# One down-projection group of the linear transformer behind the query projection, its last residual in pieces, and the quantised network's product added by GpSimd

## The chip, the core and the metric

The kernel runs on 1 core of one Trainium2 chip. A core has five engines that run their own instruction lists and meet at semaphores: TensorE (PE, matrix products; PEld is its weight load), VectorE (DVE), ScalarE (ACT), GpSimd (POOL) and SyncE (SP, here only DMA issue). The metric is the device time of one execution in microseconds (us). Lower is better.

## The reference, cut to what matters

The program is a chain of twelve sublayers on x (128 sequences of 32 tokens, width 128, so 4096 tokens). Two of them are touched.

Sublayer 2 is a linear transformer of 6 layers:

```python
for i in range(DEPTH):                       # DEPTH = 6
    xn = _layernorm(x, ln1_w[i], ln1_b[i])
    q, k, v = xn @ wq[i], xn @ wk[i], xn @ wv[i]      # split into 8 heads
    attn = softmax(q, axis=-1) @ (softmax(k, axis=-2).T @ v)
    x = attn @ wo[i] + bo[i] + x
    xn = _layernorm(x, ln2_w[i], ln2_b[i])
    hdn = xn @ w1[i]                         # 128 -> 512
    hdn = where(hdn >= 0, hdn, 0.01 * hdn)
    x = hdn @ w2[i] + x                      # 512 -> 128
```

and its result is added to the running x. Sublayer 9 is a two-layer network whose inputs, weights and biases are rounded to an integer grid: `h = relu(quant_linear(x, w1, b1)); x = x + quant_linear(h, w2, b2)`.

## The kernel before, in words

Everything is float32 except the integers of the quantised network, which are kept as bf16. The 4096 tokens are cut into CHUNKS = 8 chunks of 512 tokens (4 tiles of 128, TPC = 4).

**The linear transformer** (`linear_transformer`) is a hand-written software pipeline. Layers and chunks together make 48 items. One *step* starts an item (`now`), does the second part of attention of the item before it (`one`), the norm and feed-forward part of the one before that (`two`), and ends the feed-forward of the item three steps back (`three`). There are 48 steps that start an item and three more (48, 49, 50) that drain the pipe. The first 16 steps and the drain are written out, the other 32 run in a loop of two turns of 16 steps. Every engine has a function `step(now)` whose calls fix the order of its instructions; semaphores carry the dependences. SP only loads each layer's weights in this stage.

On PE the calls of a step are: `turn1` (4 transposes of the normed chunk into PSUM bank T), `down(three, 2)` (8 products of hidden block 2, lines L3090), `turn_keys`, `queries`, `turn_queries`, `keys`, `down(three, 3)`, `values`, `turn2`, `context`, `up` 0 and 1, `attend`, `up` 2, `down` 0, `up` 3, `down` 1, `attn_out`. All four transposing functions share the one PSUM bank T. ACT copies each of them out, and the next may write the bank only after that copy. For `turn_keys` this is the wait in its second and third line, on `s_hT1` of the item that `turn1` has just turned:

```python
def turn_keys(c):
    pe.wait_ge(s_k_exp, c.before + 1)
    if c.later(1).exists:
        pe.wait_ge(s_hT1, c.before + 2)
```

`queries` waits for the same copy, since it reads `hT1`. `down(c, 2)` waits for POOL's `leaky` (L2963), which adds two halves of the activation. POOL does it just after `apply1`, the norm of the following item (L2942, four tiles).

DVE ends the stage by adding the stream to X (`onto_x`, L3261): chunks 0 to 6 in one instruction in the last step (`now.at == 18`), chunk 7 behind everything.

**The quantised network** (`quantised_ffn`) ends in a loop over the 8 chunks. For each chunk DVE turns the hidden values of the next chunk into integers (`hidden_integers`, L2702), multiplies PE's result by the row of output scales into `product`, which has two buffers (L2706), and adds `product` to X (L2710). POOL adds the bias row to X for all 8 chunks (L2749), beginning when the rows are there. A barrier of all engines follows, and then the next cross attention (`t_cross`).

Of the kernel before, what the change touches and what calls it, by code (L numbers as in the profile page):

```python
# [13 lines left out]
ALU = mybir.AluOpType  # L14
# [11 lines left out]
TPC = 4  # L26
CHUNK = TPC * P
CHUNKS = TILES // TPC
# [150 lines left out]
def spread(ap, reps, axis):  # L179

    shape = list(ap.shape)
    shape.insert(axis, reps)
    return ap.unsqueeze(axis).to_broadcast(shape)
# [2438 lines left out]
def quantised_ffn(core, name, hT_all, quantised):  # L2622
# [7 lines left out]
    with Scope(core, name) as sc:  # L2630
# [4 lines left out]
        up, down = sc.sb("up", [P, NF * P], BF16), sc.sb("down", [P, NF * P], BF16)  # L2635
# [3 lines left out]
        diagonal, rows = sc.sb("diagonal", [P, 4, P]), sc.sb("rows", [P, 2, P])  # L2639
# [3 lines left out]
        product = sc.sb("product", [P, 2, TPC, P])  # L2643
# [4 lines left out]
        s_down, s_prod, s_bias, s_done = sc.sem("down"), sc.sem("prod"), sc.sem("bias"), sc.sem("done")  # L2648
# [5 lines left out]
        def tiles(c):  # L2654
            return X[:, c * TPC:(c + 1) * TPC]

        @block.vector
        def _(dve):
# [44 lines left out]

            def add(c):
                dve.wait_ge(s_down, c + 1)
                dve.tensor_tensor(product[:, c % 2], psum[:, D_BANK + c % 2].rearrange("p (k d) -> p k d", k=TPC),  # L2706
                                  spread(rows[:, 0], TPC, 1), ALU.mult).then_inc(s_prod, 1)
                dve.wait_ge(s_prod, c + 1)
                dve.wait_ge(s_bias, c + 1)
                dve.tensor_tensor(tiles(c), product[:, c % 2], tiles(c), ALU.add).then_inc(s_done, 1)  # L2710

            link(dve.tensor_reduce(peak[:, 0:1], quantised.peaks[:], AX.X, ALU.max))
            whole_maximum(0, 255.0)
# [19 lines left out]
            for c in range(CHUNKS):  # L2733
                if c + 1 < CHUNKS:
                    hidden_integers(c + 1)
                add(c)
            dve.wait_ge(s_done, CHUNKS)

        @block.gpsimd
        def _(pool):  # L2740
            core.clear_used(pool)
            for c in range(CHUNKS):
                pool.wait_ge(s_shift, c + 1)
                if c >= 2:
                    pool.wait_ge(s_up, NF * (c - 1))
                pool.tensor_scalar(x_int[:, c % 2], shifted[:, c % 2], ROUND, None, ALU.subtract).then_inc(s_x_int, 1)
            pool.wait_ge(s_rows, 1)
            for c in range(CHUNKS):
                pool.tensor_tensor(tiles(c), tiles(c), spread(rows[:, 1], TPC, 1), ALU.add).then_inc(s_bias, 1)  # L2749

        @block.tensor
        def _(pe):
# [52 lines left out]
def linear_transformer(core, name, stream, slots):  # L2805
# [9 lines left out]
    with Scope(core, name) as sc:  # L2815
# [36 lines left out]
        tiles = lambda ap: ap.rearrange("p (t c) -> p t c", c=P)  # L2852
# [138 lines left out]
        def _(pe):  # L2991
            def turn1(c):
                pe.wait_ge(s_norm1, c.before + 1)
                if c.later(-3).exists:
                    pe.wait_ge(s_hT2, c.before - 2)
                elif c.later(-2).exists:
                    pe.wait_ge(s_qT, 1)
                elif c.later(-1).exists:
                    pe.wait_ge(s_hT1, 1)
                for t in range(TPC):  # L3000
                    last = pe.transpose(psum[:, T_BANK, t * P:(t + 1) * P], Y1[:, t], ident)
                last.then_inc(s_turn1, 1)
# [5 lines that stand above are left out]
                else:  # L3008
                    pe.wait_ge(s_hT2, c.before - 1)
                for t in range(TPC):  # L3010
                    last = pe.transpose(psum[:, T_BANK, t * P:(t + 1) * P], k[:, c.n % 2, t * P:(t + 1) * P], ident)
                last.then_inc(s_k_turn, 1)

            def turn_queries(c):
                pe.wait_ge(s_soft, c.before + 1)
                pe.wait_ge(s_k_tok, c.before + 1)
                for t in range(TPC):
                    last = pe.transpose(psum[:, T_BANK, t * P:(t + 1) * P], q[:, c.n % 2, t * P:(t + 1) * P], ident)
                last.then_inc(s_q_turn, 1)
# [11 lines left out]
            def queries(c):  # L3031
                pe.wait_ge(s_hT1, c.before + 1)
                pe.wait_ge(s_q_less, c.before)
                for t in range(TPC):
                    last = pe.matmul(psum[:, Q_BANK, t * P:(t + 1) * P], hT1[:, t * P:(t + 1) * P], c.attn(0), start=True, stop=True)
                last.then_inc(s_qp, 1)

            def keys(c):
                pe.wait_ge(s_k_less, c.before)
                pe.matmul(psum[:, K_BANK], c.attn(P), hT1[:], start=True, stop=True).then_inc(s_kp, 1)  # L3040
# [44 lines left out]
            def down(c, f):  # L3085
                pe.wait_ge((s_early, s_late)[f // 2], c.before * 2 + f % 2 + 1)
                if f == 0 and c.later(-1).exists:
                    pe.wait_ge(s_layer, c.before)
                for t in range(TPC):
                    last = pe.matmul(psum[:, D_BANK, t * P:(t + 1) * P], hidden[:, f, t * P:(t + 1) * P], c.ffn((NF + f) * P),  # L3090
                                     start=(f == 0 and t == 0), stop=(f == NF - 1 and t == TPC - 1))
                if f == NF - 1:
                    last.then_inc(s_down, 1)

            def step(now):
                one, two, three = now.later(-1), now.later(-2), now.later(-3)
                if now.exists:
                    turn1(now)
                if three.exists:
                    down(three, 2)  # L3100
                if one.exists:
                    turn_keys(one)
                if now.exists:
                    queries(now)
                if one.exists:
                    turn_queries(one)
                if now.exists:
                    keys(now)
                if three.exists:
                    down(three, 3)  # L3110
                if now.exists:
                    values(now)
                if two.exists:
                    turn2(two)
                if one.exists:
                    context(one)
                if two.exists:
                    up(two, 0)
                    up(two, 1)
                if one.exists:  # L3120
                    for t in range(TPC):
                        attend(one, t)
                if two.exists:
                    up(two, 2)
                    down(two, 0)
                    up(two, 3)
                    down(two, 1)
                if one.exists:
                    attn_out(one)
# [65 lines left out]
        def _(dve):  # L3195
# [57 lines left out]
            def ffn_added(c):  # L3253
                dve.wait_ge(s_down, c.before + 1)
                dve.tensor_tensor(c.chunk(), tiles(psum[:, D_BANK]), c.chunk(), ALU.add).then_inc(s_layer, 1)

            def onto_x(first, last):

                at = slice(first * TPC, last * TPC)
                dve.wait_ge(s_layer, (DEPTH - 1) * CHUNKS + last)  # L3260
                dve.tensor_tensor(X[:, at], X[:, at], stream[:, at], ALU.add)  # L3261

            def step(now):
                one, two, three, following = now.later(-1), now.later(-2), now.later(-3), now.later(1)
                if two.exists:
                    attention_added(two)
                    statistics(1, two, s_stats2, s_moments2, s_norm2)
                if now.exists:
                    soften(now, Q_BANK, q, q_stat, DH, s_qp, s_q_top, s_q_less)
                if two.exists:  # L3270
                    apply2(two)
                if now.exists:
                    soften(now, K_BANK, k, k_stat, S, s_kp, s_k_top, s_k_less)
                    totals(now, q, q_stat, DH, s_q_exp, s_q_sum, s_q_inv, s_soft)
                if one.exists:
                    own_context(one)
                if following.exists:
                    statistics(0, following, s_stats1, s_moments1, s_norm1)
                if isinstance(now.i, int) and now.at == 2 * CHUNKS + 2:
                    onto_x(0, CHUNKS - 1)  # L3280
                if three.exists:
                    ffn_added(three)
                if two.exists:
                    leaky(two, 0)
                    leaky(two, 1)
                if now.exists:
                    totals(now, k, k_stat, S, s_k_exp, s_k_sum, s_k_inv, s_unit)

            statistics(0, Step(0, 0), s_stats1, s_moments1, s_norm0)
            steps(dve, step, lambda i, side: None)  # L3290
            onto_x(CHUNKS - 1, CHUNKS)
        sc.close_block()


# [229 lines left out]
```

## Time and profile before

| what | value |
|---|---|
| time, median of 3 runs | 3991.93 us (3991.15 to 3996.01) |
| the profiled execution's own time | 3982.57 us |
| its span, first to last instruction | 3980.8 us |
| PE, PEld, DVE, ACT, POOL busy | 85%, 62%, 67%, 59%, 61% |
| mean granted TensorE clock | 0.925 of full speed |
| linear transformer, first transposes to the last add | 544 us to 1336.7 us |
| quantised network, last loop | 2850.0 us to 2875.0 us |

The two stages are read apart, since another engine bounds each. A row of the timeline has the start and the length in us, the engine, the line, the operation, what it writes and reads, and in brackets the idle time before it and what ended it. Rows of one line that follow each other closely are merged, with their count behind the x; a merged row's length is from the start of the first to the end of the last. PE work overlaps, so the time that a group of products takes on PE is read from its start to the next group's start.

### The profile page before, as it was taken

What the parts mean: (1) busy time and instruction counts of PE and PEld (TensorE: products, weight loads), DVE (VectorE), ACT (ScalarE), POOL (GpSimd) and SP (SyncE); (2) the same over time, 40 slices, a digit from 0 to 9 for tenths busy, and PEclk for the clock granted to TensorE, in tenths of its full rate; (3) what the DMA queues carried; (4) which work ended last, traced back from release to release, by engine and by line L of the source; (5) the groups of instructions that cost most, each with busy time, mean ns of one, the idle gap of its engine ahead of it and who ended that gap; (6) DMA issues with size and microseconds to landing.
All of it is one profiled execution on the core that took longest, in us unless ns stands there. A gap on an engine that the chain in (4) does not pass through costs nothing. (4 is left out here: it accounts for less than half of the span.)

```text
span 3980.8 us, 119953 instructions
## 1 busy us (share of the span) xinstructions
PE 3385.2 (85%) x44674; PEld 2469.3 (62%) x44674; DVE 2670.8 (67%) x7002; ACT 2362.3 (59%) x6308; POOL 2422.3 (61%) x2724
## 2 busy tenths in 40 slices
PE   7999959999999579698698999978499999786866
PEld 5777737777777467365466777745277777453444
DVE  6888757777777523477445888857778887754655
ACT  6777736666666334386124777745577777644633
POOL 6767656776777343574425887746367676845733
PEclk9999979999999689898799999989599999887968
DMA  2111110000000122101221111110011111000023
GB/s 75 36 42 36 36 70 6 8 11 11 8 6 2 63 72 77 47 14 47 67 72 59 51 45 42 37 60 4 17 37 36 42 36 30 3 2 6 2 93 94
DMA packets 90549, 149.05 MB, mean 37 GB/s; under 512 B 10112, under 2 KB 66816, under 8 KB 89664
## 3 DMA queue, kind: packets, MB, share of 16 engines
q1 hardware_dynamic: 79936, 122.87, 9.9%
q0 software_dynamic: 10240, 20.99, 1.7%
q8 instruction: 261, 4.28, 0.4%
q14 instruction: 112, 0.92, 0.1%
HBM read 112.76 MB, written 31.06 MB: 36 GB/s over the span
## 5 line engine op out<-in xcount | busy, mean ns | idle before, releaser
L2251 POOL TENSOR_TENSOR t_cross_E<-t_cross_E,t_cross_inverse 128x1028 f32<-128x1028 f32 x128 | 243.2, 1900 | 134.8 <-DVE t_cross_inverse L2530 134.8
L2251 POOL TENSOR_TENSOR a_cross_E<-a_cross_E,a_cross_inverse 128x1028 f32<-128x1028 f32 x128 | 243.2, 1900 | 132.8 <-DVE a_cross_inverse L2530 132.8
L2477 ACT ACTIVATE t_cross_E<-t_cross_psum,t_cross_negtop 128x257 f32<-128x257 f32 x512 | 238.8, 472 | 113.5 <-DVE t_cross_negtop L2520 110.0
L2477 ACT ACTIVATE a_cross_E<-a_cross_psum,a_cross_negtop 128x257 f32<-128x257 f32 x512 | 238.8, 472 | 112.4 <-DVE a_cross_negtop L2520 103.9
L2477 ACT ACTIVATE e_cross_E<-e_cross_psum,e_cross_negtop 128x257 f32<-128x257 f32 x512 | 238.8, 472 | 111.2 <-DVE e_cross_negtop L2520 103.3
L2251 POOL TENSOR_TENSOR e_cross_E<-e_cross_E,e_cross_inverse 128x1028 f32<-128x1028 f32 x128 | 243.2, 1900 | 94.2 <-DVE e_cross_inverse L2530 94.1
L3090 PEld LDWEIGHTS l_psum<-l_ffn_w,l_hidden 128*128 128x128 f32 x1536 | 197.9, 192 | 98.0 <-issue 56.1
L3090 PE MATMUL l_psum<-l_ffn_w,l_hidden 128*128 128x128 f32 x1536 | 207.8, 278 | 19.0 <-POOL l_hidden L2963 17.9
L3083 PE MATMUL l_psum<-l_hT,l_ffn_w 128*128 128x512 f32 x384 | 200.6, 625 | 0.9 <-ACT l_hT L3139 0.9
L2520 DVE TENSOR_REDUCE t_cross_negtop<-t_cross_psum 128x2 f32<-128x514 f32 x256 | 175.8, 687 | 32.6 <-PE t_cross_psum L2337 31.7
L2520 DVE TENSOR_REDUCE a_cross_negtop<-a_cross_psum 128x2 f32<-128x514 f32 x256 | 175.4, 686 | 26.8 <-PE a_cross_psum L2332 26.4
L2520 DVE TENSOR_REDUCE e_cross_negtop<-e_cross_psum 128x2 f32<-128x514 f32 x256 | 175.6, 686 | 24.6 <-PE e_cross_psum L2332 24.5
L2942 POOL TENSOR_SCALAR l_normed<-inner,l_moments,l_rstd 128x128 f32<-128x128 f32 x192 | 149.8, 793 | 14.8 <-POOL l_rstd L2936 14.8
L2390 PE MATMUL e_cross_psum<-const_sb,e_cross_E 128*128 128x128 f32 x1024 | 154.3, 274 | 0.2
L2390 PE MATMUL a_cross_psum<-const_sb,a_cross_E 128*128 128x128 f32 x1024 | 153.4, 273 | 0.2
L2390 PE MATMUL t_cross_psum<-const_sb,t_cross_E 128*128 128x128 f32 x1024 | 153.4, 273 | 0.2
L2953 POOL TENSOR_TENSOR l_q<-l_q,l_q_stat 128x512 f32<-128x512 f32 x48 | 50.8, 1058 | 167.3 <-DVE l_q_stat L3217 167.3
L2963 POOL TENSOR_TENSOR l_hidden<-l_hidden,l_less 128x512 f32<-128x512 f32 x96 | 122.2, 1293 | 18.2 <-ACT l_hidden L3163 18.2
L1467 POOL DMA_INDIRECT slots<-hT_all,behind_place_i x64 | 61.7, 965 | 111.5 <-PE c_moe_psum L1600 61.9
L1467 POOL DMA_INDIRECT slots<-inner,a_moe_place_i x64 | 62.0, 969 | 101.6 <-PE a_moe_psum L1600 59.0
L3237 DVE TENSOR_TENSOR inner<-l_psum,inner 128x512 f32<-128x512 f32 x48 | 33.2, 692 | 132.1 <-PE l_psum L3075 132.1
L2390 PEld LDWEIGHTS e_cross_psum<-const_sb,e_cross_E 128*128 128x128 f32 x1024 | 121.2, 142 | 0.9 <-ACT e_cross_ET L2467 0.4
(754 smaller groups left out, 11124.1 us busy)
## 6 DMA issues: line engine op xcount, KB each, us to landing
a_cross_context<-context SPq DMA_DIRECT2D x32, 578.0 KB, 3.7
e_cross_context<-context SPq DMA_DIRECT2D x32, 578.0 KB, 3.7
t_cross_context<-context SPq DMA_DIRECT2D x32, 578.0 KB, 3.7
u_moe_weights<-pack_u_moe SPq DMA_DIRECT2D x1, 5633.0 KB, 16.3
slots<-l_blank SPq DMA_DIRECT2D x6, 832.0 KB, 12.2
a_moe_x_slots<-slots SPq DMA_DIRECT2D x26, 192.0 KB, 2.8
slots<-a_moe_y_slots SPq DMA_DIRECT2D x26, 192.0 KB, 2.1
c_moe_x_slots<-slots SPq DMA_DIRECT2D x26, 192.0 KB, 2.8
```

What stands on the lines that cost most here:

```text
L1467: pool.indirect_dma_start(slots.halves[g], bass.IndirectOffsetOnAxis(ap=place_i[:, k, at:at + 1], axis=0), rows[:, at], None).then_inc(s_p ...
L2251: pool.tensor_tensor(E[:, n % N], E[:, n % N], spread(inverse[:, n % 4], SK, 2), ALU.mult).then_inc(s_unit, 1)
L2390: last = pe.transpose(psum[:, (T_BANK, K_BANK)[c], g * P:(g + 1) * P], E[:, n % N, g, c * P:(c + 1) * P], ident)
L2477: act.activation(E[:, n % N, g], psum[:, g, 0:SK], ACT.Exp, bias=negtop[:, n % 2, g:g + 1], accum_out=total[:, n % 2, g:g + 1]).then_inc(s ...
L2520: dve.tensor_reduce(negtop[:, n % 2, at], psum[:, at, 0:SK], AX.X, ALU.max, negate=True).then_inc(s_top, 1)
L2942: last = pool.tensor_scalar(Y1[:, t], c.tile(t), moments[:, 0, t, 0:1], rstd[:, 0, 1, t:t + 1], ALU.subtract, ALU.mult)
L2953: pool.tensor_tensor(groups, groups, spread(q_stat[:, 2], DH, 2), ALU.mult).then_inc(s_soft, 1)
L2963: pool.tensor_tensor(hidden[:, f], hidden[:, f], less[:, f - 2], ALU.add).then_inc(s_late, 1)
L3083: pe.matmul(psum[:, U_BANKS[f % 2]], c.ffn(f * P), hT2[:], start=True, stop=True).then_inc(s_up, 1)
L3090: last = pe.matmul(psum[:, D_BANK, t * P:(t + 1) * P], hidden[:, f, t * P:(t + 1) * P], c.ffn((NF + f) * P), start=(f == 0 and t == 0), st ...
L3237: dve.tensor_tensor(c.chunk(), tiles(psum[:, C_BANK]), c.chunk(), ALU.add).then_inc(s_mid, 1)
```

## The change

It has three parts.

1. On PE `down(three, 2)` stands behind `queries(now)` instead of behind `turn1(now)`. In steps 3 to 47 all of these calls exist. No semaphore changes.
2. DVE adds the stream to X in four pieces of two chunks: three of them in steps 48, 49 and 50, the fourth at the end.
3. In the quantised network DVE no longer adds `product` to X. POOL does, and the bias of chunk c + 1 is added ahead of the product of chunk c. DVE's multiplication now waits until POOL has used the product of two chunks back.

```diff
@@ quantised_ffn
             def add(c):
                 dve.wait_ge(s_down, c + 1)
+                if c >= 2:
+                    dve.wait_ge(s_done, c - 1)
                 dve.tensor_tensor(product[:, c % 2], psum[:, D_BANK + c % 2].rearrange("p (k d) -> p k d", k=TPC),
                                   spread(rows[:, 0], TPC, 1), ALU.mult).then_inc(s_prod, 1)
-                dve.wait_ge(s_prod, c + 1)
-                dve.wait_ge(s_bias, c + 1)
-                dve.tensor_tensor(tiles(c), product[:, c % 2], tiles(c), ALU.add).then_inc(s_done, 1)
...
             pool.wait_ge(s_rows, 1)
+            pool.tensor_tensor(tiles(0), tiles(0), spread(rows[:, 1], TPC, 1), ALU.add).then_inc(s_bias, 1)
             for c in range(CHUNKS):
-                pool.tensor_tensor(tiles(c), tiles(c), spread(rows[:, 1], TPC, 1), ALU.add).then_inc(s_bias, 1)
+                if c + 1 < CHUNKS:
+                    pool.tensor_tensor(tiles(c + 1), tiles(c + 1), spread(rows[:, 1], TPC, 1), ALU.add).then_inc(s_bias, 1)
+                pool.wait_ge(s_prod, c + 1)
+                pool.wait_ge(s_bias, c + 1)
+                pool.tensor_tensor(tiles(c), product[:, c % 2], tiles(c), ALU.add).then_inc(s_done, 1)
+            pool.wait_ge(s_done, CHUNKS)
@@ linear_transformer, PE
                 if now.exists:
                     turn1(now)
-                if three.exists:
-                    down(three, 2)
                 if one.exists:
                     turn_keys(one)
                 if now.exists:
                     queries(now)
+                if three.exists:
+                    down(three, 2)
                 if one.exists:
                     turn_queries(one)
@@ linear_transformer, DVE
-                if isinstance(now.i, int) and now.at == 2 * CHUNKS + 2:
-                    onto_x(0, CHUNKS - 1)
+                if isinstance(now.i, int) and 2 * CHUNKS <= now.at < 2 * CHUNKS + 3:
+                    onto_x(2 * (now.at - 2 * CHUNKS), 2 * (now.at - 2 * CHUNKS) + 2)
...
-            onto_x(CHUNKS - 1, CHUNKS)
+            onto_x(CHUNKS - 2, CHUNKS)
```

On PE, at the head of a step in the linear transformer, before (L3001 `turn1`, L3090 `down`, L3011 `turn_keys`, L3035 `queries`, L3018 `turn_queries`, L3040 `keys`):

```order
L3001 MATMUL l_psum<-const_sb,l_normed 128x128 x4
L3090 MATMUL l_psum<-l_ffn_w,l_hidden 128x128 x4
L3011 MATMUL l_psum<-const_sb,l_k 128x128 x4
L3035 MATMUL l_psum<-l_attn_w,l_hT 128x128 x4
L3018 MATMUL l_psum<-const_sb,l_q 128x128 x4
L3040 MATMUL l_psum<-l_hT,l_attn_w 128x512
```

And now, with lines four further on:

```order
L3005 MATMUL l_psum<-const_sb,l_normed 128x128 x4
L3015 MATMUL l_psum<-const_sb,l_k 128x128 x4
L3039 MATMUL l_psum<-l_attn_w,l_hT 128x128 x4
L3094 MATMUL l_psum<-l_ffn_w,l_hidden 128x128 x4
L3022 MATMUL l_psum<-const_sb,l_q 128x128 x4
L3044 MATMUL l_psum<-l_hT,l_attn_w 128x512
```

Nothing stands between `turn1` and `turn_keys` any more, and the products of `down` are between `queries` and `turn_queries`.

On POOL, at the end of the quantised network, before (the x8 bias adds are one row):

```order
L2746 TENSOR_SCALAR q_ffn_x_int<-q_ffn_shifted 128x512 x8
L2749 TENSOR_TENSOR X<-X,q_ffn_rows 128x512 x8
L168 UNCONDITIONAL_BRANCH
L2228 UNCONDITIONAL_BRANCH
L2288 MEMSET t_cross_last_of 128x256
```

And now (L2752 adds a product, L2746 and L2749 a bias; the last seven rows before the next stage):

```order
L2752 TENSOR_TENSOR X<-q_ffn_product,X 128x512
L2749 TENSOR_TENSOR X<-X,q_ffn_rows 128x512
L2752 TENSOR_TENSOR X<-q_ffn_product,X 128x512
L2749 TENSOR_TENSOR X<-X,q_ffn_rows 128x512
L2752 TENSOR_TENSOR X<-q_ffn_product,X 128x512 x2
L168 UNCONDITIONAL_BRANCH
L2228 UNCONDITIONAL_BRANCH
```

POOL has 16 additions of a chunk where it had 8, and the last one stands directly ahead of the barrier.

On DVE, in the last steps of the linear transformer, now (L3265 is `onto_x`, L3259 the add of the feed-forward part; before, one row of 128x3584 and one of 128x512 stood around the last L3255):

```order
L3226 TENSOR_TENSOR l_ctx<-l_psum,l_unit 128x512
L3265 TENSOR_TENSOR X<-X,inner 128x1024
L3259 TENSOR_TENSOR inner<-l_psum,inner 128x512
L3254 SCALAR_TENSOR_TENSOR l_hidden<-l_hidden 128x512 x2
L3241 TENSOR_TENSOR inner<-l_psum,inner 128x512
L3231 BN_STATS l_stats<-inner 128x6 x4
L3235 BN_AGGR l_moments<-l_stats 128x2 x4
L3248 TENSOR_SCALAR l_normed<-inner,l_moments,l_rstd 128x128 x4
L3265 TENSOR_TENSOR X<-X,inner 128x1024
L3259 TENSOR_TENSOR inner<-l_psum,inner 128x512
```

Two more pieces of the same width follow, around the last L3259.

## Rows read from the trace of the kernel before

**Rows 1.** Windows: busy us (and count) of PE, PEld, DVE, ACT, POOL; granted clock

```profile
592.00:1302.00 710.00, 690.66 (x10888) 535.66 (x10886) 513.53 (x1486) 444.93 (x765) 505.98 (x586) 1.00 0.03 7
2850.00:2876.00 26.00, 14.07 (x128) 12.22 (x128) 24.47 (x25) 12.34 (x6) 15.55 (x9) 0.57 0.00 1
```

**Rows 2.** Timeline of PE in a settled step (start, length)

```profile
907.06 0.60 PE L3001 MATMUL l_psum<-const_sb,l_normed 128*128 128x128 f32 x4
908.03 1.16 PE L3090 MATMUL l_psum<-l_ffn_w,l_hidden 128*128 128x128 f32 x8 [0.38 <-POOL l_hidden L2963]
909.03 0.60 PE L3011 MATMUL l_psum<-const_sb,l_k 128*128 128x128 f32 x4
...
922.89 0.60 PE L3001 MATMUL l_psum<-const_sb,l_normed 128*128 128x128 f32 x4
```

**Rows 3.** Timeline of ACT and POOL in the same step

```profile
907.70 0.78 ACT L3139 ACTIVATE l_hT<-l_psum,l_attn_w 128x512 f32<-128x512 f32 x1 [0.80 <-PE l_psum L3001]
...
919.46 3.12 POOL L2942 TENSOR_SCALAR l_normed<-inner,l_moments,l_rstd 128x128 f32<-128x128 f32 x4 [0.31 <-POOL l_rstd L2936]
```

**Rows 4.** Timeline of PE in step 17, where POOL is early

```profile
812.71 0.60 PE L3001 MATMUL l_psum<-const_sb,l_normed 128*128 128x128 f32 x4
...
814.27 0.63 PE L3011 MATMUL l_psum<-const_sb,l_k 128*128 128x128 f32 x4
814.73 1.06 PE L3035 MATMUL l_psum<-l_attn_w,l_hT 128*128 128x128 f32 x8
815.68 0.63 PE L3018 MATMUL l_psum<-const_sb,l_q 128*128 128x128 f32 x4
...
817.00 1.05 PE L3090 MATMUL l_psum<-l_ffn_w,l_hidden 128*128 128x128 f32 x8
817.89 1.06 PE L3045 MATMUL l_psum<-l_attn_w,l_hT 128*128 128x128 f32 x8
...
827.96 0.60 PE L3001 MATMUL l_psum<-const_sb,l_normed 128*128 128x128 f32 x4
```

**Rows 5.** Timeline of PE: `turn1` of steps 3, 32 and 47

```profile
591.52 0.66 PE L3001 MATMUL l_psum<-const_sb,l_normed 128*128 128x128 f32 x4
...
1050.40 0.65 PE L3001 MATMUL l_psum<-const_sb,l_normed 128*128 128x128 f32 x4 [2.25 <-issue]
...
1285.72 0.60 PE L3001 MATMUL l_psum<-const_sb,l_normed 128*128 128x128 f32 x4
```

**Rows 6.** Timeline of DVE and POOL while the linear transformer drains

```profile
1314.06 1.27 POOL L2963 TENSOR_TENSOR l_hidden<-l_hidden,l_less 128x512 f32<-128x512 f32 x1 [8.26 <-ACT l_hidden L3163]
...
1327.83 3.89 DVE L3261 TENSOR_TENSOR X<-X,inner 128x3584 f32<-128x3584 f32 x1
...
1329.46 4.60 POOL L2963 TENSOR_TENSOR l_hidden<-l_hidden,l_less 128x512 f32<-128x512 f32 x2 [9.42 <-ACT l_hidden L3163]
...
1335.31 0.69 DVE L3255 TENSOR_TENSOR inner<-l_psum,inner 128x512 f32<-128x512 f32 x1 [3.59 <-PE l_psum L3090]
1336.04 0.69 DVE L3261 TENSOR_TENSOR X<-X,inner 128x512 f32<-128x512 f32 x1
```

**Rows 7.** Timeline of POOL in the quantised network: all eight, then two alone

```profile
2850.52 15.24 POOL L2749 TENSOR_TENSOR X<-X,q_ffn_rows 128x512 f32<-128x512 f32 x8 [12.80 <-DVE q_ffn_rows L2731]
2852.79 1.29 POOL L2749 TENSOR_TENSOR X<-X,q_ffn_rows 128x512 f32<-128x512 f32 x1
2855.71 2.26 POOL L2749 TENSOR_TENSOR X<-X,q_ffn_rows 128x512 f32<-128x512 f32 x1
```

**Rows 8.** Timeline of DVE in the quantised network

```profile
2854.55 2.28 DVE L2702 TENSOR_SCALAR q_ffn_h_int<-q_ffn_rounded 128x2048 bf16<-128x2048 f32 x1
2856.75 0.68 DVE L2706 TENSOR_TENSOR q_ffn_product<-q_ffn_psum,q_ffn_rows 128x512 f32<-128x512 f32 x1
...
2866.24 1.21 DVE L2702 TENSOR_SCALAR q_ffn_h_int<-q_ffn_rounded 128x2048 bf16<-128x2048 f32 x1
...
2874.34 0.69 DVE L2710 TENSOR_TENSOR X<-q_ffn_product,X 128x512 f32<-128x512 f32 x1
```

More of the change, by code:

```diff
@@ L2736, in _ @@
                 add(c)
-            dve.wait_ge(s_done, CHUNKS)
         @block.gpsimd
```

## The prediction

> **What bounds the kernel.** I read the windows first. In the linear transformer PE is busy 690.66 of 710 us at the full granted clock, 2.4 GHz, and no other engine passes 514 us [rows 1]: there a microsecond of PE is a microsecond of the kernel. In the last loop of the quantised network it is DVE, busy 24.47 of 26 us, with POOL at 15.55 [rows 1]. So the first part of the change is judged on PE, the third on the port that DVE and POOL share.
>
> Then the timeline of one settled step of the linear transformer. It lasts 922.89 - 907.06 = 15.83 us, and its visible flaw is the wait of PE for POOL's `l_hidden` ahead of `down`, 0.38 us [rows 2]. What the reader is to see is that another wait lies under it. `turn_keys` starts at 909.03, but it may not start before ACT has copied out what `turn1` left in the same PSUM bank. ACT begins that at 907.70 and takes 0.78 us, to 908.48 [rows 3]. So in the settled step POOL is the later releaser, and ACT's copy is only half a microsecond behind.
>
> Step 17 shows the same head with POOL early. `down` is issued at once behind `turn1`, and `turn_keys` still starts 814.27 - 812.71 = 1.56 us after `turn1` [rows 4]. The eight products of `down` fill that hole. This step lasts 827.96 - 812.71 = 15.25 us, the shortest of the stage: it is what PE needs when nobody but ACT's copy holds it up.
>
> **Part 1, `down` behind `queries`.** It removes nothing; PE issues the same products. The hole of 1.56 us between `turn1` and `turn_keys` stays, since its cause is ACT and not POOL, and is now empty. The products of `down` become a piece of their own behind `queries`. Eight of them take 817.89 - 817.00 = 0.89 us from their start to the next group's [rows 4]. Against that, `turn_queries` now has them as cover for ACT's copy of the keys: in step 17 it came 815.68 - 814.73 = 0.95 us behind `queries`, where eight products need 0.89, so 0.06 is saved [rows 4]. The new step is 15.25 + 0.89 - 0.06 = 16.08 us if PE sets it.
>
> It does, for nothing else comes late. POOL's `l_hidden` is now needed 2 us later. `queries`, and all that DVE and POOL do behind it, start at 1.56 + 0.46 = 2.02 us into the step (0.46 from `turn_keys` to `queries` [rows 4]), not at 909.03 + 0.44 - 907.06 = 2.41. POOL's norm for the next `turn1` ended at 919.46 + 3.12 = 922.58, 0.31 us before it was used [rows 3]; it gains up to 0.39 from the earlier start and 0.25 from the longer step. DVE's norm for `turn2` is earlier too while PE comes to it later. So the loop over DVE and POOL, which set the step before, has slack, and PE's own list sets it.
>
> From step 3 to step 47 there are 44 intervals, 1285.72 - 591.52 = 694.20 us, 15.78 each [rows 5]. In that sum are starts of the loop body that no order on PE changes: 2.25 us of issue at step 32 [rows 5], and I put as much as 1.1 us more on the entries at steps 3 and 16 (an estimate: half of the one seen). The new sum is 44 x 16.08 + 3.35 = 710.9, so +16.7 us, and the 45th step of this kind adds 0.3: **+17.0 us**. In the drain `turn_keys` gets ahead of `down`, but the next step then waits for POOL's deviation, which nothing moved: 0.
>
> Bounds: if the hole is 1.62 and DVE or POOL take back what they gain, the step is 16.2 us, +22. If the step rises only from the settled 15.83 by the difference of the hole and its two old fillings, 15.83 - (909.03 - 907.06) + 1.56 + 0.89 - 0.22, with 0.22 for small waits before `turn_queries` and `turn2` that go, it is 16.09 again; with each of these waits taken at 0.3 it would be 15.9, +9.
>
> **Part 2, the residual in pieces.** DVE's 3.89 us add over seven chunks runs from 1327.83, and POOL's two `l_hidden` additions beside it take 4.60 us from 1329.46, where one alone took 1.27 [rows 6]. PE's last `down` and DVE's last two adds hang on them. With pieces of two chunks, 0.69 + (3.89 - 0.69) / 6 = 1.22 us each [rows 6], the third piece ends at 1329.05, before POOL begins. POOL's pair then takes between 2 x 1.27 = 2.54 and, since its second half waits for ACT, some 3.3 us: 1.3 to 2.1 earlier; I take 1.3. The last piece is 1.22 long and not 0.69, +0.5. The pieces in steps 48 and 49 lie where DVE waits for POOL and ACT. Sum **-0.7 us**, between -1.5 and +0.6 (cover gone in step 48, no gain at the end).
>
> **Part 3, GpSimd adds the product.** Per chunk DVE loses an add of 0.69 us [rows 8], and POOL gains one of 1.29 [rows 7]. That alone would suit DVE, but the two engines hinder each other. The integer step takes DVE 2.28 us while POOL works and 1.21 alone; the multiplication that reads PSUM takes 0.68 us with POOL at work [rows 8]; POOL's addition takes 1.29 alone and 2.26 when an integer step falls on it [rows 7]. So each integer step costs POOL 2.26 - 1.29 = 0.97 us.
>
> Before, POOL's eight additions were over at 2850.52 + 15.24 = 2865.76, and DVE ended undisturbed at 2874.34 + 0.69 = 2875.03. Now POOL has 16 additions, one behind the other. Rows of it overlap by some 0.05, so 16 x 1.24 = 19.8 us, and seven integer steps fall among them (DVE's multiplication waits for POOL's add of two chunks back, which keeps the two in step): 7 x 0.97 = 6.8. The first product is ready before POOL wants it. At the end two additions wait on a multiplication for 0.3 at most. End: 2850.52 + 26.6 + 0.3 = 2877.4 to 2877.9, against 2875.03. The next stage begins behind the barrier, and all of it moves: **+2.7 us**. Bounds: no interference, 16 x 1.24, is -4.7; every addition at 2.26 is 36.2 us, +11.7. I stay near the middle, since integer steps fall on just under half of the additions.
>
> The Trainium skill has a rule against this part: GPSIMD Engine Reference, 4.1 Engine selection, puts an elementwise operation with two inputs on VectorE, GpSimd being about twice as slow. The trace agrees: 1.29 to 0.69 us, a factor of 1.87 [rows 7, 8]. It also says (SBUF — State Buffer, the section on the two separate sides) that the port pair of the two engines is locked for a whole instruction and the other blocks. By it each integer step would cost POOL its full 1.21 us and not 0.97, an estimate of 1.7 us more; the row says a little less than the rule.
>
> **Sum.** 17.0 - 0.7 + 2.7 = +19.0 us on the profiled execution's 3982.57, which is 4001.6. The runs' median of 3991.93 lies 9.4 us above that execution; the difference is carried over unchanged: **4010.9 us**, 0.48% slower. Less than 0.2%, 8 us, could not be told from no change here.
>
> **Rivals.**
> (a) *The loop through POOL sets the step, and `down` leaves it.* For: PE waits for POOL's `l_hidden` in every settled step [rows 2]; with `down` behind `queries`, the queries start 0.4 us earlier, and the chain DVE, POOL, `down`, `turn_keys`, `queries`, DVE gets shorter by 1.0 us. If the hole behind `turn1` then counted for nothing, all steps would come down to step 17's 15.25: 44 x 15.25 + 3.35 - 694.2 = -20 us, with the other parts 3974 us. It decides if `turn_keys` starts less than about 1.2 us behind `turn1`. Against: step 17, where POOL is early and the hole is 1.56 all the same [rows 4]. 6 in 100.
> (b) *The price is there but small.* The step comes to 15.9 us (+5 to +9) and part 3 to its lower bound because POOL and DVE fall apart in time: 3991.93 + 7 - 0.7 - 3 = 3995. For: a settled step holds small waits I can't see one by one. 12 in 100.
> (c) *The granted clock.* PE's idle share rises from 3% to some 8%; in the quantised network, where PE is busy about half the time, the clock stood at 0.57 [rows 1]. At 1.2 GHz a step's 15 us of PE work nearly double, so even three steps are +45: about 4055 us. Against: in step 17's head, and in the 2.25 us at step 32, no row slows. 4 in 100.
> (d) The change does what it says by the instruction order, so a change without effect is only (b).
>
> **Chances and range.** My forecast has 78 in 100. Its own range is +10 to +25 us, from the step's bounds and part 3's nearer ones. To hold 8 in 10 the range takes in some of (b): 3998 to 4023. Faster 0.07: (a) and a bit. Same 0.13: (b) and the lower edge. Slower 0.80.
>
> **What would show it.** In the new profile `turn_keys` should start 1.55 to 1.6 us behind `turn1` with PE idle about 1.0 us before it, released by ACT's `l_hT`; no wait for POOL's `l_hidden` ahead of `down`; `turn1` every 16.0 to 16.15 us, the same in both halves of the loop body. POOL's two additions in the drain should take about 3.3 us together and the last one of the quantised network end near 2877.7 plus the shift. I am wrong if the step is below 15.9 us, if PE's hole is filled, or if the clock's row for 592 to 1302 falls below 1.00.

## The result, and the profile after

| | before | after |
|---|---|---|
| time, median of 5 runs | 3991.93 us (3990.57 to 3996.01) | 4015.23 us (4012.67 to 4016.09) |
| ratio to before, 95% interval | | 1.0054 (1.004 to 1.0069) |
| the profiled execution's own time | 3982.57 us | 4015.23 us |
| settled step of the linear transformer | 15.83 / 15.65 us | 16.07 us |
| `turn1` of step 3 to `turn1` of step 47 | 694.20 us | 712.67 us |
| that `turn1` to the end of the last add | 51.01 us | 50.66 us |
| POOL's first addition to its end, quantised network | 24.51 us (DVE's end) | 26.63 us |

The change costs 23.3 us; 19.0 had been forecast. The three lower rows explain +18.5, -0.35 and +2.1 of the profiled executions. These two executions lie 32.7 us apart, since the one of before was 9.4 us under its median. Most of the rest is in stages with no edit (`c_self` +4.7, `retention` +4.0, `t_cross` +3.3); e3, which does not touch `c_self` either, has it 3.4 us longer than before. I do not read it.

One profile of each kernel is also a thin basis for the first two of these, 694.20 to 712.67 and 51.01 to 50.66. The profile of before is the fastest of its kind in both. Where nothing in the linear transformer differs from before, the 44 intervals take 694.20 us in before, 698.65 in e3 and 695.51 in e8 (the experiments are below), and the stretch behind them takes 51.01, 52.57 and 52.46.

The timeline of PE in a settled step after the change (start, length, engine, line; in brackets the idle time and what ended it):

```profile
916.14 0.60 PE L3005 MATMUL l_psum<-const_sb,l_normed 128*128 128x128 f32 x4
917.70 0.63 PE L3015 MATMUL l_psum<-const_sb,l_k 128*128 128x128 f32 x4 [0.96 <-ACT l_hT L3143]
918.17 1.06 PE L3039 MATMUL l_psum<-l_attn_w,l_hT 128*128 128x128 f32 x8
919.06 1.06 PE L3094 MATMUL l_psum<-l_ffn_w,l_hidden 128*128 128x128 f32 x8
919.95 0.60 PE L3022 MATMUL l_psum<-const_sb,l_q 128*128 128x128 f32 x4
...
932.21 0.60 PE L3005 MATMUL l_psum<-const_sb,l_normed 128*128 128x128 f32 x4
```

These answer to [rows 2]. The wait for POOL's `l_hidden` is gone; in its place is one of 0.96 us for ACT's `l_hT`. `turn_keys` still starts 1.56 us behind `turn1`, as in [rows 4]. `down(three, 2)` now takes 0.89 us of its own behind `queries`, 919.06 to 919.95. The step is 932.21 - 916.14 = 16.07 us, in both halves of the loop body.

Windows of after (columns as in [rows 1]): the stage, a piece of step 32, a piece of the drain, and the last loop of the quantised network.

```profile
593.00:1321.00 728.00, 681.46 (x10885) 533.04 (x10885) 520.68 (x1485) 439.44 (x765) 505.37 (x586) 1.00 0.03 7
1064.40:1067.80 3.40, 3.40 (x18) 3.40 (x18) 0.85 (x2) 0.60 (x1) 1.65 (x2) 0.50 0.00 0
1325.00:1333.00 8.00, 6.12 (x162) 3.82 (x166) 4.45 (x9) 1.97 (x3) 0.67 (x1) 0.79 0.01 2
2880.00:2906.00 26.00, 11.99 (x123) 10.24 (x121) 15.49 (x15) 11.64 (x6) 26.00 (x16) 0.63 0.01 1
```

PE's idle share in the stage rose from 2.7% to 6.4%, and the granted clock is still 1.00 as a mean of the stage. It was not 1.00 all the time: for 3.4 us of step 32 it was 0.50, the 1.2 GHz level, and it fell once more in the drain. In the last loop the bound moved from DVE, busy 24.47 of 26 us [rows 1], to POOL, busy all 26.

The timeline of DVE and POOL there, one chunk of the settled part and the end, answers to [rows 7, 8]:

```profile
2886.52 1.28 POOL L2749 TENSOR_TENSOR X<-X,q_ffn_rows 128x512 f32<-128x512 f32 x1
2886.68 0.69 DVE L2708 TENSOR_TENSOR q_ffn_product<-q_ffn_psum,q_ffn_rows 128x512 f32<-128x512 f32 x1 [1.24 <-POOL X L2752]
2887.28 1.61 DVE L2702 TENSOR_SCALAR q_ffn_h_int<-q_ffn_rounded 128x2048 bf16<-128x2048 f32 x1
2887.76 2.27 POOL L2752 TENSOR_TENSOR X<-q_ffn_product,X 128x512 f32<-128x512 f32 x1
2889.98 1.28 POOL L2749 TENSOR_TENSOR X<-X,q_ffn_rows 128x512 f32<-128x512 f32 x1
...
2903.97 2.48 POOL L2752 TENSOR_TENSOR X<-q_ffn_product,X 128x512 f32<-128x512 f32 x2
```

An addition with an integer step on it takes 2.27 us, one with only the multiplication on it 1.28. DVE waits 1.24 us in each chunk for POOL to free a `product` buffer.

### The profile page after: what moved, and what is told of

The parts are those of the page before. It is cut to its first block and busy times, and to the rows that moved or that the text cites. A ratio compares the mean times of both kernels' runs of the same rounds, so it can differ in the third digit from the quotient of the medians.

```text
span 4013.4 us, 119960 instructions
## 1 busy us (share of the span) xinstructions
PE 3390.0 (84%) x44673; PEld 2470.8 (62%) x44674; DVE 2671.4 (67%) x6996; ACT 2357.3 (59%) x6308; POOL 2431.1 (61%) x2732
## 5 line engine op out<-in xcount | busy, mean ns | idle before, releaser
L2520 DVE TENSOR_REDUCE a_cross_negtop<-a_cross_psum 128x2 f32<-128x514 f32 x256 | 175.4, 686 | 26.9 <-PE a_cross_psum L2332 26.6
L2390 PEld LDWEIGHTS t_cross_psum<-const_sb,t_cross_E 128*128 128x128 f32 x1024 | 121.2, 142 | 1.0 <-ACT t_cross_ET L2467 0.4
```

The source lines that it names most:

```text
L2390: last = pe.transpose(psum[:, (T_BANK, K_BANK)[c], g * P:(g + 1) * P], E[:, n % N, g, c * P:(c + 1) * P], ident)
L2520: dve.tensor_reduce(negtop[:, n % 2, at], psum[:, at, 0:SK], AX.X, ALU.max, negate=True).then_inc(s_top, 1)
```

## The experiments

Kernels with the same number under "before there" ran on one chip together with those runs of before; the ratio is to them.

| kernel | median us | before there | ratio (95%) | settled step us |
|---|---|---|---|---|
| e1 order alone | 4011.69 | 3994.37 | 1.0045 (1.0031 to 1.0058) | 16.06 |
| e2 pieces alone | 3988.34 | 3994.37 | 0.9987 (0.9977 to 0.9996) | 15.83 / 15.65 |
| e3 POOL adds alone | 3997.02 | 3994.37 | 1.0008 (0.9999 to 1.0017) | not touched |
| e4 block 2 on DVE | 3978.73 | 3994.37 | 0.9958 (0.9945 to 0.9972) | 15.25 |
| e5 filler of transposes | 4071.98 | 4003.64 | 1.017 (1.0156 to 1.0184) | 16.06 to 19.84 |
| e6 `turn1` ahead | 4034.63 | 4003.64 | 1.0073 (1.0059 to 1.0087) | 16.33 / 16.14 |
| e7 e4 with pieces | 3988.61 | 4003.64 | 0.9961 (0.9947 to 0.9975) | 15.25 |
| e8 no bias adds | 3990.41, one run | 4003.64 | none | not touched |
| e9 filler, one product | 4014.95 | 3990.01 | 1.006 (1.0048 to 1.0072) | 16.07 |
| e10 16 empty instructions | 4073.68 | 3990.01 | 1.0212 (1.0198 to 1.0227) | 16.06 to 19.92 |
| e11 e7 with the order | 4010.89 | 3990.01 | 1.0052 (1.0039 to 1.0065) | 16.06 |
| e12 12 empty instructions | 4025.33 | 4004.2 | 1.005 (1.0033 to 1.0067) | 16.06 |

**e1, e2, e3: each part by itself.** The edits are the three parts of the diff, one at a time.

> Kernel before with part 1 alone (down block 2 behind the query projection). Theory A (the hole between turn1 and turn_keys is ACT's copy and is now empty): turn1 every 16.07 us as in the changed kernel, linear transformer +18 to +19 us, total +17 to +20 us. Theory B (part 1 costs less and the rest of the +23 us comes from part 3's effect on later stages): total +10 us or less.

> Kernel before with part 2 alone (residual in four pieces). Theory A: POOL's last two additions take about 3.3 us together and not 4.6, the stage ends 0.7 us earlier; total within 1 us of before, not to be told from no change. Theory B (the pieces hold up DVE in the drain): the stage ends up to 1 us later.

> Kernel before with part 3 alone (GpSimd adds the product). Theory A (POOL's 16 additions in a row and the port shared with DVE's integer steps): last loop of the quantised network +2 to +3 us, total +2 to +3. Theory B (later stages, above all the cross attention behind it, are slower because of it): total +6 us or more. Theory C (DVE is freed and this pays): -2 us or better.

Part 1 alone gives +17.3 us and the step of 16.06: the cost is the order on PE. Part 2 gives -6.0 by the medians. Its own rows show less: from `turn1` of step 47 to the last add it takes 49.08 us, against 51.01 in before and 52.57 in e3, so -1.9 to -3.5. The other 2.5 to 4 us are in no row that it touches. Part 3 gives +2.6, with an interval that just takes in none; its last loop has the same 26.6 us as after. The three sum to +14, and together they measured +23. By the ratios (+0.45, -0.13, +0.08% against +0.54%) the 0.14% between them is within the intervals, so I do not call it an interaction.

**e4: take POOL's lateness away and leave `down` in the hole.** On before: hidden block 2 goes through DVE, as 0 and 1 do; ACT writes it in one copy, and POOL keeps block 3 alone.

```diff
@@ POOL                                    @@ DVE, behind totals(now, k, ...)
-                    leaky(two, 2)          +                    leaky(two, 2)
@@ PE down                                  @@ ACT raw
-  s_early / s_late by f // 2               -                if f >= 2:
+  s_early for f < 3, s_late for f == 3     +                if f == 3:
```

> Kernel before, down left where it was, but the activation of hidden block 2 made by DVE (after its key totals, where it waits for PE) as for blocks 0 and 1, so that ACT writes one copy of it and POOL handles block 3 alone. Theory A (the 0.53 us hole behind turn1 was POOL's lateness, and ACT's copy of 1.56 us is the next limit): a step falls from 15.74 us on average to 15.3 to 15.5, total -11 to -20 us. Theory B (the loop over DVE sets the step): DVE's 0.69 us more make a step as long or longer, total 0 to +10 us.

This is the version that beats both kernels, by 0.42% under before. Its head of a step, in the timeline of PE:

```profile
920.01 0.60 PE L3000 MATMUL l_psum<-const_sb,l_normed 128*128 128x128 f32 x4
920.44 1.06 PE L3092 MATMUL l_psum<-l_ffn_w,l_hidden 128*128 128x128 f32 x8
921.57 0.63 PE L3010 MATMUL l_psum<-const_sb,l_k 128*128 128x128 f32 x4
```

`down` follows at once, `turn_keys` still comes at 1.56 us, and every undisturbed step takes 15.25. So the wait for POOL that one sees in [rows 2] was worth 0.4 to 0.6 us a step, and was to be had without emptying the hole. The edit also takes a copy from ACT and an addition from POOL; how much of the gain belongs to each was not tried.

**e7 and e11: with and without the order, where POOL is never late.** e7 is e4 with part 2; e11 adds part 1 to it.

> Block 2's activation on DVE (as in e4_block2_dve) and the residual in pieces (part 2), the rest as before. Theory A (the two gains are in different places and add up): step 15.25 us, total -15 to -22 us on before. Theory B (part 2's gain in its own run was chance): as e4_block2_dve, -15.6 us within 3.

> e7_block2_dve_pieces with part 1 on top (down block 2 behind the queries). There PE never waits for POOL at the head of a step, so the price of the place stands alone. Theory A (0.89 us of work leaves a place where it was free): step 15.25 to 16.05 us, +35 to +38 us on e7_block2_dve_pieces, so +19 to +22 us on before. Theory B (part 1's price is tied to POOL's lateness): +17 us or less on e7_block2_dve_pieces.

The step goes from 15.25 to 16.06, +0.81, where the prediction's terms have 0.89 - 0.06 = 0.83. e7 cannot be told from e4. Against their own runs of before, e7 is 15.0 us faster and e11 20.9 us slower: where POOL is never late, the order costs about 36 us and not 17, since before had already paid POOL's lateness. In e11 the hole is there although POOL is early:

```profile
934.67 0.60 PE L3000 MATMUL l_psum<-const_sb,l_normed 128*128 128x128 f32 x4
936.23 0.63 PE L3010 MATMUL l_psum<-const_sb,l_k 128*128 128x128 f32 x4 [0.96 <-ACT l_hT L3141]
```

**e5, e9, e10, e12: is the hole free?** Each puts something between `turn1` and `turn_keys` of after: e5 eight transposes into a bank that is free then, e9 one 128x512 product into it, e10 and e12 no work but 16 or 12 semaphore increments.

```diff
@@ e5: after turn1(now)
+                for n in range(2):
+                    for t in range(TPC):
+                        pe.transpose(psum[:, Q_BANK, t * P:(t + 1) * P], Y1[:, t], ident)
@@ e9
+                pe.matmul(psum[:, Q_BANK], ident, Y1[:].rearrange("p t c -> p (t c)"), start=True, stop=True)
@@ e10; e12 has range(12)
+                for n in range(16):
+                    pe.sem_inc(passed_pe, 1)
```

> The changed kernel with eight more transposes on PE between turn1 and turn_keys in each of the 48 steps (they read turn1's source, write the query bank and are overwritten by the queries; 0.88 us of PE work). Theory A (PE stands idle there until ACT's copy lands): the step stays at 16.07 us within 0.05, total as the changed kernel within 3 us, so +17 to +26 us on before. Theory B (the step is the length of PE's own list, or the products of down got dearer at their new place): 16.95 us a step, total +60 us and more on before.

> The changed kernel with one more product of 128x512 on PE between turn1 and turn_keys (two matmuls and two weight loads with one wait: some 0.9 us of PE work in 5 instructions, where e5_filler had 0.88 us in 17); overwritten by the queries. Theory A1 (the place is idle; e5_filler's loss was the supply of PE's instructions, seen as 0.9 to 2 us gaps for which the profile names no releaser): settled step 16.07 us, few such gaps, total +15 to +35 us on before. Theory A2 (work there is not free): +60 us or more.

> The changed kernel with 16 instructions that only raise an unused count, on PE between turn1 and turn_keys: no PE work, but as many more instructions in a step as e5_filler. Theory A1 (instruction supply): the 0.9 to 2 us gaps of e5_filler come back, total +40 to +70 us on before. Theory B1 (PE work in the place is what e5_filler paid for): as the changed kernel, +17 to +26 us.

> The kernel after with 12 semaphore increments in the hole between turn1 and turn_keys, where the run before it had 16 and cost 1.6% over the kernel after. PE issues some 498 instructions a step (966 products and weight loads and 31 others in two steps of the trace), so this makes it about 510 and the 16 made it 514. Theory A, a boundary: the instruction list comes in packets of 16384 bytes, two in a step, and what fits in them costs nothing, so the step stays 16.07 us, few issue gaps, 0 to +8 us over the kernel after (ratio to before 1.005 to 1.008). Theory B, a price for each instruction: 12/16 of 59 us, +44 us over the kernel after, ratio 1.016 to 1.018, with some 25 issue gaps ahead of the small products of attend. A value between 1.009 and 1.015 would fit neither.

e5 missed what the theory of a free hole said: +1.7%. e9 shows that the theory holds all the same: about 0.9 us of work in each step, the settled step is still 16.07 us, and the ratio to before is 1.006, where after has 1.0054. What e5 had besides work was instructions, and e10, with instructions and no work, costs more than e5. The timeline of PE in e10, at three steps one after the other (`attend` is L3075, 128 products a step):

```profile
691.78 1.25 PE L3075 MATMUL l_psum<-l_qT,l_ctx 32*32 32x32 f32 x125
694.31 0.25 PE L3075 MATMUL l_psum<-l_qT,l_ctx 32*32 32x32 f32 x3 [1.27 <-issue]
...
709.33 1.27 PE L3075 MATMUL l_psum<-l_qT,l_ctx 32*32 32x32 f32 x126
711.90 0.24 PE L3075 MATMUL l_psum<-l_qT,l_ctx 32*32 32x32 f32 x2 [1.30 <-issue]
...
726.92 1.27 PE L3075 MATMUL l_psum<-l_qT,l_ctx 32*32 32x32 f32 x127
730.10 0.21 PE L3075 MATMUL l_psum<-l_qT,l_ctx 32*32 32x32 f32 x1 [1.92 <-issue]
```

The reader is to see the counts: the wait falls behind 125, 126, 127 products. It moves on by one product, a weight load and a matmul, in each step. Counting all of PE's records, a step of e10's written-out part has 510, and the waits lie at records 15441, 15953 and 16465: 512 apart each time. Up to the second turn of the loop the other waits of over 0.6 us in e10 (but one, in step 2) and in e5 lie whole multiples of 512 from these, within two records. Those of after, e1, e2, e3 and e11 (18257 in all five) and e9 are whole multiples of 512 apart too, but half of 512 away from those of e10, which nothing here explains. In the loop's second turn they come back at the same places of the body. So PE can run dry at every 512th record, and in its longest waits within a settled step the ones ahead of it are the dense small products of `attend`. Not every such place has a wait: steps 4 and 6 of e10 have none.

A second loss comes with the first. In each step of e5 and e10 from step 2 on that takes over 19 us (five and eight of them) the granted clock also fell from 2.4 to 1.2 GHz for a few microseconds. So what e5 and e10 lost is not the waits alone.

e12's result fits its theory A (ratio 1.005, no wait of that kind in the loop's steady part), but the reason that it gives, fewer than 512 in a step, is not the whole one. Its loop steps have 511 records, so the 512th stays at nearly the same place of each step, and that place is not in `attend`; e10's have 515, and it drifts slowly through the end of `attend`. Before and after have 494 in the written-out steps and 499 in the loop, so the place moves on by 18 or 13 records a step; besides the loop's second turn such waits show in steps 13 to 15 alone, one in before and in after, two or three in e1, e2 and e3. e9's loop has 503, with waits of 1.3 to 1.4 us in the steps 21, 34 and 37, and of 0.36 us in step 18.

That this is the supply of instructions is argued: the queue named "instruction" moved 1.46 MB in 89 packets in some 44 steps of before, two of 16 KB in a step. It was not tried by itself, nor is it shown why a wait at a given record comes in one execution and not in the next.

**e6: another order that fills the hole.** On after, `turn1` of the next item stands ahead of `attn_out`, whose eight products cover ACT's copy.

```diff
-                if now.exists:
-                    turn1(now)
...
+                if now.later(1).exists:
+                    turn1(now.later(1))
                 if one.exists:
                     attn_out(one)
```

> The changed kernel with the next item's turn1 ahead of the attention's output projection, so that real work (0.89 us) lies in the hole. Theory A: the step falls from 16.07 to 15.5 to 15.9 us (15.2 by PE's list, but POOL's norm is ready only some 15.5 us into the step and DVE gets the output projection later), total +0 to +13 us on before. Theory B (the hole is not what costs): the step stays at 16.07, total +20 us or more.

A miss. The hole is gone, but the step is 16.33 and 16.14 us. The timeline of PE and DVE:

```profile
843.69 0.66 PE L3005 MATMUL l_psum<-const_sb,l_normed 128*128 128x128 f32 x4 [0.47 <-POOL l_normed L2946]
844.18 1.06 PE L3079 MATMUL l_psum<-l_attn_w,l_aT 128*128 128x128 f32 x8
845.30 0.63 PE L3015 MATMUL l_psum<-const_sb,l_k 128*128 128x128 f32 x4
...
845.27 0.69 DVE L3242 TENSOR_TENSOR inner<-l_psum,inner 128x512 f32<-128x512 f32 x1 [3.79 <-PE l_psum L3079]
```

DVE gets the attention's result 1.58 us behind `turn1`, where e7 has 934.30 - 934.10 = 0.20. All that DVE and POOL do behind it is later, and PE waits for POOL's norm at the next `turn1`. The order moved the bound to the loop over DVE and POOL. The total, +31 us on before, is what theory B gave, but not for its reason, since the hole is filled.

**e8: how much of part 3 is POOL's second addition.** Part 3 on before, with POOL's bias adds left out.

```diff
-            pool.tensor_tensor(tiles(0), tiles(0), spread(rows[:, 1], TPC, 1), ALU.add).then_inc(s_bias, 1)
...
-                if c + 1 < CHUNKS:
-                    pool.tensor_tensor(tiles(c + 1), tiles(c + 1), spread(rows[:, 1], TPC, 1), ALU.add).then_inc(s_bias, 1)
...
-                pool.wait_ge(s_bias, c + 1)
```

> Part 3 alone, with POOL's eight additions of the bias row left out (the down bias is missing from the output). Theory A (POOL's 16 additions in a row are the length of the last loop): the loop is then DVE's, 8 integer steps of 1.2 to 2.3 us and 8 multiplications of 0.68, 16 to 20 us from the rows' arrival to the last addition where part 3 alone takes 26.6. Theory B (each DVE-POOL round trip of product and buffer is what costs): the loop stays above 23 us.

Its POOL, in the timeline:

```profile
2868.30 14.43 POOL L2748 TENSOR_TENSOR X<-q_ffn_product,X 128x512 f32<-128x512 f32 x7 [14.99 <-DVE q_ffn_product L2708]
2883.14 1.26 POOL L2748 TENSOR_TENSOR X<-q_ffn_product,X 128x512 f32<-128x512 f32 x1 [0.41 <-DVE q_ffn_product L2708]
```

The stage, from PE's first weight load to the first instruction of the next one, takes 59.47 us against 67.78 with part 3 whole (e3) and 65.71 before. From the rows' arrival to the last addition it is 18.4 us where e3 takes 26.7, inside theory A's 16 to 20. With eight additions POOL is no longer the bound: it waits for DVE's last product. So what costs is 16 additions on one engine. Without the bias, adding the product on POOL would gain 65.71 - 59.47 = 6.2 us; that is an upper bound, since here nobody adds the bias. The single time of 3990.41 us is not read.

## Why the prediction was right, and where its terms were off

**The order, and the sum's largest term.** Predicted 16.08 us for the step, measured 16.07, in both halves as said; the hole is 1.56 us with 0.96 idle. That POOL is not the cause is shown by e11, where POOL is early and the hole stays, and that PE stands idle in it by e9, where work in it costs nothing. That it is ACT's copy of `l_hT` is read from the wait in the code and from the releaser in the profile; no run makes the copy shorter or gives `turn_keys` a bank of its own. The 44 intervals came to 712.67 us against 710.9. 44 x 16.07 is 707.1, so the disturbed steps hold 5.6 us and not the 3.35 that I carried over from before: 17.57 at step 14, where a wait of 1.30 us for issue stands behind 123 of `attend`'s products, and 17.95 and 17.96 at steps 31 and 32. The wait of 1.72 us for issue at the start of step 32 is the excess of step 31. The excess of step 32 itself is the clock, as the timeline of PE shows:

```profile
1062.62 0.65 PE L3005 MATMUL l_psum<-const_sb,l_normed 128*128 128x128 f32 x4 [1.72 <-issue]
1064.23 0.94 PE L3015 MATMUL l_psum<-const_sb,l_k 128*128 128x128 f32 x4 [0.96 <-ACT l_hT L3143]
1064.97 1.91 PE L3039 MATMUL l_psum<-l_attn_w,l_hT 128*128 128x128 f32 x8
```

Behind the wait for issue and the hole, 1.72 and 0.96 us idle with `turn1` alone between them, eight products take 1.91 us and not 1.06, and the window 1064.40 to 1067.80 shows 0.50. Before had a longer wait at this place, 2.25 us [rows 5], no hole behind it, no fall, and a step of 15.30. e1 and e11, with the order, have 17.96 and 17.75; e9, with the hole filled, has no fall and 16.12. A full hole does not always prevent it: e2 and e7, which keep `down` there, fell too, with 16.60 and 17.13.

That was the mis-sized term, +2.3 us. "Starts of the loop body that no order on PE changes" was the sentence that failed: one of these waits is no start of the body at all, the empty hole adds a fall of the clock to another, and they differ between executions. For the last reason the 18.5 us are themselves uncertain. With the order of before the 44 intervals take 694.2 to 698.7 us (before, e2, e3, e8, mean 696.4), with that of after 712.7 to 715.3 (after, e1, e11, mean 714.2): +17.8, where +16.7 was forecast.

**The pieces and the drain.** Their row in the first table was forecast at -0.4 (-0.7 for the pieces, +0.3 for the 45th step, nothing else from the order) and measured -0.35. That this agrees is luck: both terms were too small, and before's profile is the fastest of its kind here. POOL's last two additions, in after:

```profile
1349.96 1.56 POOL L2967 TENSOR_TENSOR l_hidden<-l_hidden,l_less 128x512 f32<-128x512 f32 x1 [8.47 <-ACT l_hidden L3167]
1351.71 1.26 POOL L2967 TENSOR_TENSOR l_hidden<-l_hidden,l_less 128x512 f32<-128x512 f32 x1 [0.19 <-ACT l_hidden L3167]
...
1354.95 1.23 DVE L3265 TENSOR_TENSOR X<-X,inner 128x1024 f32<-128x1024 f32 x1
```

They take 3.01 us from the first start to the last end, where 3.3 was said and 4.60 stood before [rows 6]: 1.6 gained, less the 0.5 for the longer last piece. In other profiles with the residual in one instruction the pair takes longer than in before, and most in e1, whose timeline of DVE and POOL has:

```profile
1349.95 3.88 DVE L3261 TENSOR_TENSOR X<-X,inner 128x3584 f32<-128x3584 f32 x1
1350.75 5.43 POOL L2963 TENSOR_TENSOR l_hidden<-l_hidden,l_less 128x512 f32<-128x512 f32 x2 [8.47 <-ACT l_hidden L3163]
```

e1 and after differ in this stage by the pieces alone, and agree up to the last step's `turn2` within 0.02 us. From `turn1` of step 47 to the last add they take 53.61 and 50.66 us: the pieces gain 2.95. e2 against before gives 1.9 and against e3 3.5, and e7 against e4 gives 53.33 - 50.05 = 3.3. So the pieces are worth 1.9 to 3.5 us, outside the bound of 1.5 that was stated for them.

The order takes part of this back, where 0 was said for the drain. e2 has the pieces without the order, in 49.08 us; after, with it, needs 50.66. The difference is the granted clock. Behind a wait of 2.19 us for DVE's norm, where before waits 0.77, `context` takes 1.94 us where it took 1.08 in the settled step:

```profile
1326.88 0.81 PE L3032 MATMUL l_psum<-const_sb,l_normed 128*128 128x128 f32 x4 [2.19 <-DVE l_normed L3248]
1327.62 1.94 PE L3060 MATMUL l_psum<-l_v_own,l_k_tok 128*32 128x128 f32 x32
```

From this `turn2` to that of the last step it is 15.82 us in after and 14.44 in e2, where the same stretch (1310 to 1318) shows a clock of 1.00. That is 1.4 of the 1.6 us between them. The fall does not always come: e1, e5, e11 and e12 have it too, but e9 and e10 have the same wait of 2.19 us, no fall, and 14.24 and 14.25 us from this `turn2` to the last one. No profile with the order of before has it there.

**GpSimd adds the product.** Predicted +2.7, measured +2.12. The additions took 26.63 us; 26.6 was the sum. Seven long and nine short ones, as counted. The 0.3 us allowed at the end for a late multiplication did not come: the last two additions follow at 2.48 us together. An addition with an integer step on it is lengthened by 2.27 - 1.28 = 0.99 us, where 0.97 was taken from the rows of before; that is again less than the 1.21 us of an integer step alone. DVE pays too: its integer step takes 1.44 to 1.69 us beside POOL, 2.28 before [rows 8], and 1.21 alone.

**What is left.** The own terms as measured make +20.2 us (18.5 - 0.35 + 2.1), the medians +23.3. The ratio's interval is 16 to 28 us, so the 3 us are not resolved. The total lies close to the forecast partly because errors cancel: the order costs more than was said, in the loop and in the drain, and the pieces gain more.

**The rivals.** (a), the loop through POOL with no hole, needed `turn_keys` less than 1.2 us behind `turn1`; it stayed at 1.56. What was true in it, that POOL's lateness is worth something, e4 cashed in. (b) fell with the step of 16.07 and part 3's +2.1. (c) did not come in the settled steps: the clock's row for the stage is 1.00 at 6.4% idle. It did come in small, once in step 32 for 1.9 us and once in the drain for 1.4 us.

## What to carry to other kernels

Behind the latest releaser of a wait look for the second latest: here POOL's lateness hid a copy by ACT half a microsecond behind it, and moving the waiting group away exposed a hole that the group had filled for nothing. Make the late engine earlier (e4) rather than send the work elsewhere. And when an operation goes from one engine to another, count what the receiving one already does in that loop: the addition that cost DVE 0.69 us took POOL 1.3 to 2.3.

## What the runs showed of the hardware that was not expected

- In these kernels TensorE lost up to 2 us, mostly 1.3 to 1.6, at places 512 records of its own apart, when dense small products stood ahead of them. Sixteen empty instructions a step cost 1.6% over after (1.0212 to 1.0054), falls of the clock included; twelve cost nothing that can be measured. Such waits have only "issue" as a releaser, and a few instructions more in the loop body (e9, e10, e12) move them.
- The granted clock fell from 2.4 to 1.2 GHz for short stretches after single waits of PE: in 1325 to 1333 of after, mean 0.79, behind 2.19 us; in 1064.4 to 1067.8 of after, 0.50, behind 1.72 and 0.96 us; and in 1069.5 to 1073.5 of e12, mean 0.51, behind 3.74 us of issue, where eight products took 1.92 us and not 1.06. A wait of the same length does not always do it: 2.19 us in e9 and e10 and 2.25 us in before were followed by no fall. In the settled steps of after, each with a wait of 0.96 us, it stayed at 1.00.
